# Attention of an eight-group block rebuilt: exponentials read from PSUM, probabilities split in SBUF and turned by DMA, all engines on one written order

## What is computed

```python
y = x * rsqrt(mean(x * x) + 1e-6) * rms_w
y = einsum('bsm,cm->bsc', y, w_in)           # q: 32 heads of 64, k and v: 8 groups of 64
q, k = rope(q), rope(k)
qk = einsum('bghsd,bgxpd->bghsp', q, k) * 64 ** -0.5
attn = softmax(where(causal, qk, -inf))
o = einsum('bghsp,bgxpd->bghsd', attn, v)
y = x + einsum('bsc,mc->bsm', o, w_out)
x1 = layernorm(x + y)
out = layernorm(x1 + ternary(x1) @ (ternary(w) + variation).T)
```

## Time and profile before

| | |
|---|---|
| median of 3 runs | 1410.89 us |
| profiled execution | 1411.72 us, its span 1409.9 us |
| granted TensorE clock, mean | 0.984 |
| busy: TensorE, VectorE, ScalarE, GpSimd | 91%, 84%, 79%, 60% |
| moved by DMA | 61.82 MB |

### The profile page before, as it was taken

How to read it: one execution, slowest core, us unless ns; L and a number is a source line. 1 busy time by engine, 2 the same in 40 slices (tenths; PEclk the granted TensorE clock), 3 DMA queues, 4 the chain that set the end, 5 groups by cost and what they waited for, 6 DMA issues and landing times.

```text
span 1409.9 us, 25319 instructions
## 1 busy us (share of the span) xinstructions
PE 1289.2 (91%) x7328; PEld 755.6 (54%) x7328; DVE 1182.2 (84%) x3062; ACT 1107.8 (79%) x2327; POOL 852.2 (60%) x904
## 2 busy tenths in 40 slices
PE   4689898999989999999989999999989999898886
PEld 2455555555645555555645555555555555454554
DVE  4688887989898898988898898989898898888976
ACT  5768778788888888788888888788887788687764
POOL 1356666386746765386646766386646766786566
PEclk9799999999999999999999999999999999999998
DMA  6101111021101201021101211021101211110012
GB/s 202 26 20 48 56 31 32 27 57 46 39 21 47 59 28 31 25 59 45 38 22 42 59 33 31 24 61 43 37 24 28 71 35 44 56 42 27 19 36 82
DMA packets 45164, 61.82 MB, mean 44 GB/s; under 512 B 10465, under 2 KB 27105, under 8 KB 45025
## 3 DMA queue, kind: packets, MB, share of 16 engines
q1 hardware_dynamic: 45024, 60.20, 14.4%
HBM read 34.74 MB, written 4.46 MB: 28 GB/s over the span
## 4 chain that ended last, share of the span: by engine, by line
PE 53%; POOL 10%; DVE 9%; issue 9%; ACT 8%; DMA 7%; SPq 3%; POOLq 0%; DVEq 0%; ACTq 0%
PE s L1167 11%; PE x L1179 11%; PE t L1223 11%; PE x L1207 7%; PE ot L1138 6%; DMA spread<-recip_rows 6%; PE ot L1136 5%; ACT prob L831 4%; DVE prob L1010 3%; DVE prob_lo L1102 2%; ACT prob_hi L799 2%; POOL o_raw L766 2%; SPq L574 1%; POOL o_lo L772 1%; SPq L590 1%
## 5 line engine op out<-in xcount | busy, mean ns | idle before, releaser
L799 ACT ACTIVATE prob_hi<-t 128x512 f16<-128x512 f32 x576 | 340.3, 592 | 139.4 <-PE t L1223 134.5
L1102 DVE SCALAR_TENSOR_TENSOR prob_lo<-t,prob_hi 128x512 f16<-128x512 f32 x576 | 394.2, 685 | 59.7 <-ACT prob_hi L799 53.9
L831 ACT ACTIVATE prob<-prob,neg_max 128x896 f32<-128x896 f32 (+7 forms) x512 | 391.9, 767 | 9.3 <-DVE neg_max L1010 7.3
L1167 PE MATMUL s<-k_t,q_t 128*128 128x512 f16 (+3 forms) x1536 | 349.5, 329 | 32.7 <-DVE neg_max L1010 12.1
L1223 PE MATMUL t<-ident,prob 128*128 128x128 f32 x2304 | 350.3, 275 | 6.8 <-ACT prob L831 6.7
L1010 DVE CUSTOM_DVE_ANT_0 prob<-s,mask,score_scale 128x512 f32<-128x512 f32 (+3 forms) x512 | 319.8, 643 | 41.1 <-PE s L1167 23.9
L1223 PEld LDWEIGHTS t<-ident,prob 128*128 128x128 f32 x2304 | 289.4, 142 | 105.8 <-ACT prob L831 14.0
L1138 PE MATMUL ot<-prob_lo,v_sb 128*128 128x512 f16 x576 | 220.7, 383 | 30.2 <-DVE prob_lo L1102 29.1
L1136 PE MATMUL ot<-prob_hi,v_sb 128*128 128x512 f16 x576 | 220.1, 382 | 1.5 <-DVE o_raw L1083 0.9
L1167 PEld LDWEIGHTS s<-k_t,q_t 128*128 128x128 f16 x1536 | 137.7, 99 | 123.1 <-DVE neg_max L1010 37.6
L772 POOL TENSOR_TENSOR o_lo<-o_raw,o_hi 128x256 f16<-128x256 f32 x128 | 86.2, 674 | 194.1 <-ACT o_hi L906 192.5
(11 more groups left out here) (105 smaller groups left out, 1816.5 us busy)
## 6 DMA issues: line engine op xcount, KB each, us to landing
swapped<-flat SPq DMA_DIRECT2D x320, 64.0 KB, 2.0
spread<-recip_rows SPq DMA_DIRECT2D x128, 128.0 KB
recip_rows<-turned SPq DMA_DIRECT2D x512, 0.5 KB
raw<-L_attn_w_in SPq DMA_DIRECT2D x8, 768.0 KB, 4.2
raw<-L_attn_w_out SPq DMA_DIRECT2D x8, 512.0 KB, 3.7
out<-acc SPq DMA_DIRECT2D x16, 256.0 KB, 2.0
acc<-L_attn_x SPq DMA_DIRECT2D x3, 1024.0 KB, 9.8
acc<-L_attn_x SPq DMA_DIRECT2D x4, 256.0 KB, 3.1
```

The source lines that it names most:

```text
L799: act.activation(prob_hi[:, u % 2, :], t_ps[u % 2][:, :], ACT.Copy, scale=P_SCALE).then_inc(prob_hi_done, 1)
L831: act.activation(row, row, ACT.Exp, bias=neg_max[:, kk % 4, h:h + 1], scale=-1.0, accum_out=total[:, kk % 4, h:h + 1]).then_inc(ex_done, 1)
L1102: dve.scalar_tensor_tensor(out=prob_lo[:, u % 2, :], in0=t_ps[u % 2][:, :], scalar=P_SCALE, in1=prob_hi[:, u % 2, :], op0=ALU.mult, op1=AL ...
L1167: mm = pe.matmul(s_ps[:, off:off + cols], q_t[:, h, s * P:(s + 1) * P], k_t[:, part, keys:keys + cols], start=(part == 0), stop=(part == 1))
```

## The change

The scores go to four banks (`s`, two steps of two banks). The causal mask becomes a 16-bit matmul of 128 columns that adds to the last 128 keys of a row. VectorE only reduces the scores in PSUM to a maximum (`mx`) and scales it (`nm`); ScalarE takes the exponential straight from PSUM (`ex`) with scale and bias read per partition. A row's four sums get a reciprocal times 2^14 (`rc`); ScalarE multiplies the exponentials by it into a 16-bit `part_hi` in SBUF (`ph`), VectorE computes `part_lo` (`pl`) from the exponentials and `part_hi`, both in SBUF. SyncE issues DMA transposes of both (`th`, `tl`: one transfer for four heads where s is under 4, for two heads elsewhere, 192 of each), and TensorE multiplies the turned parts by the values (`pv`). The turning matmuls, both copies from `t`, the way of the reciprocals through DRAM and the multiplication by `spread` go. GpSimd now makes both `o_hi` and `o_lo` (`oh`). The feed-forward uses three bf16 parts in place of two 32-bit ones. Every engine takes its events from one list, sorted by the numbers in `PLACES`; the work on q, k, v and the output stays as it was.

```diff
 if e[0] == "sc":                              # TensorE
-                            wait(pe, max_done, g, STEPS_MADE, n - 1)
+                    if n >= 2:
+                        wait(pe, ex_done, heads_through(n - 2))
...
+                            if c == s // HALF:
+                                pe.matmul(s_ps[:, off + cols - P:off + cols], ident_h[:, :], later[:, :],
+                                          start=False, stop=False)
...
-                        for h in range(HG):
-                            mm = pe.transpose(t_ps[u % 2][:, h * P:(h + 1) * P],
-                                              prob_row(s, h)[:, j * P:(j + 1) * P], ident[:, :])
...
+                    pe.matmul(ot_ps[R % 2][:, :], values, hi[:, :, j, :], start=(j == 0), stop=False)
+                    for heads in groups_of(s):
+                        n = GROUP_OF[B, s, heads[0]]
+                        wait(pe, lo_in[n % LANES], 16 * (n // LANES + 1))
+                    pe.matmul(ot_ps[R % 2][:, :], values, lo[:, :, j, :], start=False, stop=(j == s)
+                              ).then_inc(pv_done, 1)
...
 VectorE
-                            dve.tensor_tensor_reduce(out=prob_row(s, h)[:, c * BANK:c * BANK + cols],
-                                                     in0=s_ps[:, off:off + cols], in1=mask[:, seen:seen + cols],
...
+                    dve.tensor_reduce(out=row_max[:, n % 4, 0:heads], in_=scores, axis=AX_X, op=ALU.max
+                                      ).then_inc(row_max_done, 1)
...
+                    dve.tensor_scalar(neg_max[:, n % 4, 0:heads], row_max[:, n % 4, 0:heads],
+                                      score_scale[:, G % 2:G % 2 + 1], -1.0, ALU.mult, ALU.mult).then_inc(max_done, 1)
...
-                        dve.scalar_tensor_tensor(out=prob_lo[:, u % 2, :], in0=t_ps[u % 2][:, :], scalar=P_SCALE,
-                                                 in1=prob_hi[:, u % 2, :], op0=ALU.mult, op1=ALU.subtract
-                                                 ).then_inc(prob_lo_done, 1)
+                    dve.scalar_tensor_tensor(out=part(part_lo, B, s, h), in0=prob_row(B, s, h),
+                                             scalar=recip[:, R % 4, h:h + 1], in1=part(part_hi, B, s, h),
+                                             op0=ALU.mult, op1=ALU.subtract).then_inc(part_lo_done, 1)
...
 ScalarE
-                        act.activation(prob_hi[:, u % 2, :], t_ps[u % 2][:, :], ACT.Copy, scale=P_SCALE
-                                       ).then_inc(prob_hi_done, 1)
...
-                            act.activation(row, row, ACT.Exp, bias=neg_max[:, kk % 4, h:h + 1], scale=-1.0,
-                                           accum_out=total[:, kk % 4, h:h + 1]).then_inc(ex_done, 1)
+                    wait(act, part_lo_done, R * HG + h + 1 - PROBS)
...
+                    act.activation(prob_row(B, s, h), s_ps[:, off:off + cols], ACT.Exp,
+                                   bias=neg_max[:, n % 4, i:i + 1], scale=score_scale[:, G % 2:G % 2 + 1],
+                                   accum_out=total[:, R % 4, h:h + 1]).then_inc(ex_done, 1)
...
+                    wait(act, recip_done, R + 1)
...
+                    act.activation(part(part_hi, B, s, h), prob_row(B, s, h), ACT.Copy,
+                                   scale=recip[:, R % 4, h:h + 1]).then_inc(part_hi_done, 1)
...
 GpSimd
-                            pool.tensor_tensor(o_raw[:, :, :], o_raw[:, :, :], spread[:, kk % 2, :, :], ALU.mult
-                                               ).then_inc(o_t_done, 1)
+                    pool.tensor_copy(o_hi[:, R % 2, :, :], o_raw[:, R % 2, :, :]).then_inc(o_hi_done, 1)
...
 SyncE
+                    wait(sp, done, R * HG + heads[-1] + 1)
+                    for after in TURNED_PLACES[R][1]:
+                        wait(sp, pv_done, row_end(after))
+                    wait(sp, lanes[n % LANES], 16 * (n // LANES))
+                    sp.dma_start_transpose(turned_group(turned, n), group_part(tile, n)).then_inc(lanes[n % LANES], 16)
```

More of the change, by code:

```diff
@@ L48, with steps_of @@
+TILES = 2 * NT
 FIRST_TILES = 8
 POOL_TILES = 14
+RING = 2
+PROBS = 8
+PARTS = 6 * KEYS
+TURNED = 19
+LANES = 4
+X_KINDS = ("pj", "vt", "op", "norm", "tern", "ffn", "nw", "no")
 def first_unit(s):
     return s * (s + 1) // 2
[L56 to L65, removed]
+def steps_of(s):
+    return [(0, 1), (2, 3)] if s < HALF else [(h,) for h in range(HG)]
@@ new lines, in groups_of, with step, step_of, heads_through @@
+def groups_of(s):
+    return [tuple(range(HG))] if s < HALF else [(0, 1), (2, 3)]
+def step(B, s, i):
+    return B * STEPS_MADE + SCORED[s] + i
+def step_of(B, s, h):
+    return step(B, s, h // 2 if s < HALF else h)
+def heads_through(n):
+    B, n = divmod(n, STEPS_MADE)
+    s = max(s for s in range(NT) if SCORED[s] <= n)
+    return (B * NT + s) * HG + steps_of(s)[n - SCORED[s]][-1] + 1
+def unit(B, s, j):
+    return B * UNITS + first_unit(s) + j
+def chunk(B, half, c):
+    return (2 * B + half) * 3 + PLACE[c]
@@ L68, in swaps, with k_slots @@
+def k_slots(B, half):
+    return 0 if half else HALF + HALF * (B % 2)
 def swaps(n):
     return sum(32 if m % 3 == 0 else 64 for m in range(n, -1, -2))
[L73 to L88, removed]
@@ L249, in first_plan, with ring_places @@
-def first_plan():
-    plan = Plan(1, 0)
-    plan.ahead[0] = list(FIRST)
-    return plan.number()
-def seq_block(nc, x, w_in, w_out, rms_w, ffn_w, ffn_r, cos, sin, ident_d, tri_d, row_d, out):
-    B, S, D = x.shape
-    TT = B * S // P
+def ring_places(sizes, capacity):
+    places, at = [], 0
+    for n, size in enumerate(sizes):
+        if at + size > capacity:
+            at = 0
+        over = [m for m in range(n) if places[m][0] < at + size and at < places[m][0] + sizes[m]]
+        places.append((at, [m for m in over if m > over[-1] - LANES]))
+        at += size
+    return places
@@ L259, in seq_block, with event_order @@
+def event_order():
+    placed = []
+    for G in range(NG):
+        for kind, events in pass_events(G).items():
+            for at, e in zip(PLACES[G][kind], events):
+                placed.append((at, len(placed), (kind,) + e))
+    return [e for _, _, e in sorted(placed)]
+def seq_block(nc, x, w_in, w_out, rms_w, ffn_w, ffn_r, cos, sin, ident_d, tri_d, out):
+    B_IN, S, D = x.shape
+    TT = B_IN * S // P
     KC = D // P
@@ L261, in seq_block @@
     WC = QC + 2 * DH
-    NQ = NG * QC
-    assert B == 2 and S == NT * P and D == BANK and WC <= BANK
+    assert B_IN == 2 and S == NT * P and D == BANK and WC <= BANK and TT == TILES
     LAST = NG - 1
-    first, opening = first_plan(), body_plan(True, False)
-    middle, final = [body_plan(False, False) for _ in range(1, LAST)], body_plan(False, True)
-    plans = [first, opening] + middle + [final]
-    first.base, first.past = 0, None
-    for past, plan in zip(plans, plans[1:]):
-        plan.base, plan.past = past.base + len(past.x), past
+    order = event_order()
+    x_index = {e: n for n, e in enumerate(e for e in order if e[0] in X_KINDS)}
+    x_events = list(x_index)
     x_v = x.rearrange("b (t p) d -> p (b t) d", p=P)
@@ L481, in chunk, with wait_x_full @@
-        def chunk(b, half, c):
-            return 3 * (2 * b + half) + PLACE[c]
-        def scored(b, s, h=0, c=0):
-            return b * SCORED[NT] + SCORED[s] + score_steps(s).index((h, c))
-        STEPS_MADE = 2 * SCORED[NT]
-        def unit_of(u):
-            b, u = divmod(u, UNITS)
-            s = max(s for s in range(NT) if first_unit(s) <= u)
-            return b, s, u - first_unit(s)
-        def over_bodies(eng, one):
-            for g, plan in enumerate(plans, -1):
-                one(g, plan)
+        def wait_x_full(eng, e):
+            wait(eng, x_full, x_index[e] + 1)
+            return x_ps[x_index[e] % RING]
@@ L503, in scratch, with turned_group, heads_before, row_end @@
+        def turned_group(tile, n):
+            B, s, heads = GROUPS[n]
+            at, cols = TURNED_PLACES[B * NT + s][0] * HG * P, (s + 1) * P
+            some = tile[:, at + heads[0] * cols:at + (heads[-1] + 1) * cols]
+            return some.rearrange("p (n q) -> p n q", q=P)
+        def heads_before(n):
+            return sum(len(heads) for _, _, heads in GROUPS[:n])
+        def row_end(R):
+            B, s = divmod(R, NT)
+            return unit(B, s, s) + 1
         def scratch(n):
-            return prob[:, n * BANK:(n + 1) * BANK]
+            return prob[:, n, BANK:KEYS]
```

1752 lines of the change are left out of this document (1022 added, 730 removed), and 145 rows, old and new, of tables (FIRST, LAYER, PROJECT, SCORES).

## The result

The changed kernel takes 1462.59 us (median of 4 runs, 1461.15 to 1465.62) against 1411.04 us before in the same session: a ratio of 1.0363, 95% interval 1.033 to 1.0395. It is slower, as forecast, and 12.6 us over the forecast of 1450.

A forecast was written before the change was run, and what follows sets the result against it. TensorE bounds the old kernel's middle; after the change VectorE: 1160 us work plus 186 us waiting, 1346; 1215 in the middle at 96.2% gives 1263, plus 185 us ends, span 1448, time 1450 us; range 1262 to 1590.

The forecast's parts named there:

- The bound: Whole kernel: TensorE no longer the bound; VectorE would be above 90% busy, with 1346 us of work and waiting.
- the turns cost nothing: Rival, chance 0.25: GpSimd's work falls beside VectorE's PSUM reading, so low parts don't wait; 1273 us.
- the sign: Whole kernel: slower, 38 us over the profiled execution; chance of slower 0.63, faster 0.31, same 0.06.
- The low parts: VectorE's 512 low parts, both inputs in SBUF, wait for GpSimd's instructions: 0.36 us each, 186 us.
- The price without a collision: VectorE's low parts uncontended: 0.22 us fixed plus 1.044 ns a column, 421 us for 512.
- The small instructions: VectorE's 384 small scalings and 128 second reciprocal steps: each priced as the 169 ns reciprocal, 87 us.
- The frame: The fullest engine's work in the middle fills 96.2% of it, plus 185 us of ends.
- The feed-forward, counted at nothing: Three-part feed-forward in the last stretch: no added TensorE time counted, as it stands under VectorE's work there.
- the forecast's 826 us: The 384 DMA transposes at 183 GB/s, 0.175 us a 128 x 128 block: hidden under VectorE.
- its other two estimates: DMA transposes by the skill's pages: 380 to 430 us, or 6.0 ms at 1309 ns a block one after the other.
- the transposes become the bound: Rival, chance 0.15: DMA transposes at 0.4 us a block take 1843 us, about 1950 us with the ends.
- the split doesn't relieve TensorE: Rival, chance 0.07: TensorE's order waits for whole rows of four heads, idle time replaces turning work; 1411 us.

The follow-up runs named there:

- e1: Changed kernel with GpSimd's rotary products and low parts turned into memsets that write but do not read: 1313.2 us, 0.9315 of the kernel before.
- e6: Changed kernel with the low parts made but not turned, 192 of the 384 transposes left out: 1468.5 us, 1.0415 of the kernel before.
- e4: Changed kernel with the 128 two-column neg_max instructions split into 256 of one column: 1455.6 us, 1.0330 of the kernel before.
- e8: Changed kernel with all 384 neg_max instructions moved from VectorE to ScalarE: 1414.9 us, 1.0022 of the kernel before.
- e10: Changed kernel with neg_max and the factor 2^14 moved to ScalarE, GpSimd's rotary products and q/k low parts halved: 1411.0 us, 0.9995 of the kernel before.

## Why the prediction was right

**The bound.** VectorE takes TensorE's place, at 91% (forecast: above 90%); e1 took away most of GpSimd's reads, and half of its work with them, and came out 7% under the kernel before. That is nearly the condition of the rival "the turns cost nothing", 1273 us, and it gave 1313: the sign of the change hangs on VectorE's collisions with GpSimd.

**The luck.** It does not hang on those of the low parts alone, as the prediction had it. Its sum breaks even at 0.29 us a low part, and 0.236 was measured. With nothing else changed its own sum would then give 1160 + 121 = 1281 us of work, a span of (1281 - 131) / 0.962 + 185 = 1380 and a time of 1382 us: faster by 2%. By this sum, what made the change slower is a second collision that the prediction did not have, 78 us on the small instructions, which brings it to 1463 (with 1359 us of work for the 1329 measured, and less idle time than there was). The bound and the collision of the low parts were foreseen; the sign, and a time within 1%, owe it to two errors that cancel.

**The low parts.** Mechanism right, price too high: 0.236 us each, 121 us in all, where I took 0.36 and 186. My row was the mean of the 32 low parts of the input weights, 984 ns. The same group stands at 864 ns after the change, 0.24 over its bare 0.62 us: the row was the right one, but it met GpSimd more often in the kernel before (21 of the 32 stood over 0.06 us above the bare price there, 12 after); why, was not tried. The price without a collision (0.22 us + 1.044 ns a column) held.

**The small instructions.** The step that failed is "the 384 small scalings and 128 second steps of the reciprocal cost as the 169 ns reciprocal: 87 us". They took 109.9 + 55.3 = 165 us. A reciprocal does not collide, a scaling of several columns does; none of the rows read from the kernel before has one. The two errors cancel: 607 + 87 us forecast for low parts and small ones, 529.7 + 165.2 measured, and VectorE's total 1329 for 1346.

**The frame.** VectorE does not reach TensorE's 96.2% in the middle: 93.6% in the stretch above (163.73 of 175). Over the span it stands idle 134.5 us where the forecast had 1448 - 1346 = 102. So 17 us less work and 32 us more idle make the span 1463.8 for 1448. The idle time is partly the order's: 31.7 us ahead of the maxima and 25.4 us ahead of the reciprocal, each waiting on another engine.

**The rest.** The maximum took 357 us (366 forecast), an exponential 1201 ns at 1024 columns and 452 at 128, so 0.836 ns a column again, a high part 767 ns (767 by the forecast's price), ScalarE 1128 (1155). GpSimd has 910 us where the prediction left it at 852: its products are longer too (1436 ns where 1.28 us was read). TensorE has 1161 us for 1095. The feed-forward, counted at nothing, is not the reason: its matmuls take 44.8 us, 53.0 before. A score matmul of 512 columns takes 417 ns for 382, at a granted clock of 0.91 for 1.00 in the middle; since scores waited 195.5 us for exponentials, no run shows that this cost time, and none tried it. The transposes stayed hidden at 0.186 us a block; the forecast's 826 us are 0.179 a block (it wrote 0.175), and its other two estimates, 380 to 430 us for all and 6.0 ms, stand against twice 428 us. The rival "the transposes become the bound" fell with e6. The rival "the split doesn't relieve TensorE" fell with e1, which has the same order on TensorE and took 1313 us, and with the idle time ahead of the value products, 9.9 us in all in the changed kernel.

## What to carry to other kernels

When work moves to VectorE, ask of each instruction whether it reads the SBUF twice, or scales more than one column from SBUF to SBUF, and what GpSimd does at that time: such instructions can wait out whole GpSimd instructions, and GpSimd theirs. Before moving work off the fullest engine, look for the hand-over that the move adds: here a step of 0.43 us moved to another engine came back as waiting, and only the moves without a new hand-over gave time. And when a forecast comes out, redo its sum with the measured terms: here the term that was watched would have given the other sign.

## What the runs showed of the hardware

- VectorE's scalings of two to five columns collide with GpSimd (431 to 560 ns in the mean with whole GpSimd instructions; in e1 some still wait out memsets, which only write), those of one column (202 ns, the longest of 512 in e4 0.22 us) do not, and the reciprocal of four or five (171 to 183 ns in the mean) shows none in its mean.
- VectorE's low parts, with both inputs in the SBUF, take turns with GpSimd's reading instructions (excess 0.236 us in the mean) and not with its memsets (112 in e1, none more than 0.05 us over the bare price).
- A GpSimd instruction behind a low part loses time too: 1.86 us where another of its kind takes 1.27, behind a low part of 768 columns.
- A 16-bit DMA transpose from SBUF to SBUF cost 0.186 us of all 16 DMA engines per 128 x 128 block, 176 GB/s.
- TensorE's granted clock in the stretch from 585 us, a mean over the two levels of 2.4 and 1.2 GHz: 1.00 at 168 us of work in 175, 0.91 at 141 us after the change, but 0.97 at 151 us in e1 and 0.98 at 144 us in e10. The busy share alone does not order these; what the clock costs here was not tried by itself.
- A neg_max of one or two columns takes ScalarE 286 ns in the mean, beside whole GpSimd instructions (e8) and beside halves (e10).
